# Value matmuls of attention issued one query tile later, behind the next tile's scores

## The reference

```python
x = x + mamba(_layernorm(x), ...)
x = x + _L0_ffn_ref(_layernorm(x), w_gate, w_up, w_down)   # silu(x wg) * (x wu), then wd
x = x + _L0_attn_b_ref(_layernorm(x), W)
x = x + _L0_ffn_ref(_layernorm(x), w_gate, w_up, w_down)

def _L0_attn_b_ref(x, W):          # x: (8, 2048, 1024)
    kv = x @ W.T
    K, V = (kv[..., :d], kv[..., d:])
    scores = jnp.einsum('bqd,bkd->bqk', x, K) + mask     # causal
    attn = jax.nn.softmax(scores, axis=-1)
    return x + jnp.einsum('bqk,bkd->bqd', attn, V)
```

## Time and profile before

| | |
|---|---|
| time, median of 2 runs | 3401.28 us (3397.95 to 3404.62) |
| the profiled execution | 3400.72 us |
| its span, slowest core (core 4) | 3399.1 us; cores 3373.0 to 3399.1 |
| mean granted TensorE clock, core 4 | 0.785 of 2.4 GHz |
| PE, DVE, ACT, POOL busy | 59%, 28%, 23%, 10% of the span |
| DMA | 233.31 MB, mean 69 GB/s |

### The profile page before, as it was taken

One profiled execution on the slowest core, in us unless ns is written; L12 is line 12 of the kernel. 1 busy time (PEld: TensorE's weight loads), 2 busy tenths in 40 slices (PEclk: granted clock), 3 DMA queues, 4 the chain that ended last, 5 costly groups with the idle time before them and its releaser, 6 DMA issues.

```text
span 3399.1 us, 29902 instructions; the slowest of 8 cores (3373.0 to 3399.1 us)
## 1 busy us (share of the span) xinstructions
PE 2007.9 (59%) x9275; PEld 982.9 (29%) x9432; DVE 956.2 (28%) x1617; ACT 776.6 (23%) x1196; POOL 323.4 (10%) x404
## 2 busy tenths in 40 slices
PE   0355555555555530664958678119767486859587
PEld 0233333333333210321423233114333232324232
DVE  3234444444444430011112120444322121211120
ACT  0244545445454423200101010110000110101010
POOL 0211212112121210021000000000000000000000
PEclk9576676676766755886988989559888698989889
DMA  7200000000000029334030212450211503030303
GB/s 239 78 13 25 1 25 1 25 25 1 25 1 25 22 93 287 112 113 144 8 109 8 78 47 62 156 180 2 75 62 50 182 26 99 16 108 1 112 12 96
DMA packets 69851, 233.31 MB, mean 69 GB/s; under 512 B 8450, under 2 KB 8578, under 8 KB 67652
## 3 DMA queue, kind: packets, MB, share of 16 engines
q10 hardware_dynamic: 35712, 112.21, 9.9%
q1 hardware_dynamic: 27460, 91.92, 8.8%
q0 software_dynamic: 6528, 27.27, 2.0%
HBM read 170.55 MB, written 60.82 MB: 68 GB/s over the span
## 4 chain that ended last, share of the span: by engine, by line
PE 38%; DMA 21%; DVE 13%; ACT 9%; issue 8%; DVEq 4%; POOLq 2%; POOL 2%; ACTq 2%; SPq 0%
PE ps_s L975 15%; DMA arena<-wd_c 6%; PE ps_s L941 5%; DVEq L143 4%; DMA arena<-xs 3%; PE ps_s L1045 3%; PE ps L1322 3%; PE ps L1045 3%; POOLq L143 2%; ACT L679 2%; POOL arena L560 2%; DVE arena L516 2%; PE ps L759 2%; PE ps_s L1266 2%; PE ps_s L1223 2%
## 5 line engine op out<-in xcount | busy, mean ns | idle before, releaser
L975 PE MATMUL ps_s<-arena 128*128 128x512 bf16 x2256 | 506.6, 385 | 10.8 <-DVE arena L328 8.6
L584 PE MATMUL ps_s<-arena 128*128 128x256 bf16 x1024 | 213.7, 397 | 339.1 <-ACT arena L508 336.0
L318 PE MATMUL ps<-arena 128*128 128x128 bf16 x512 | 63.5, 307 | 481.8 <-DVE arena L307 481.8
L975 PEld LDWEIGHTS ps_s<-arena 128*128 128x128 bf16 x2304 | 227.9, 99 | 288.1 <-issue 25.0
L1045 PE MATMUL ps_s<-arena 128*128 128x512 bf16 x752 | 207.9, 396 | 149.2 <-DMA arena<-wd_c 95.4
L266 ACT ACTIVATE arena<-arena 128x1024 bf16<-128x1024 f32 x64 | 67.6, 1056 | 910.8 <-DMA arena<-xs 820.9
L584 PEld LDWEIGHTS ps_s<-arena 128*128 128x128 bf16 x1024 | 137.2, 138 | 408.5 <-issue 356.1
L941 PE MATMUL ps_s<-arena 128*128 128x512 bf16 x752 | 172.3, 390 | 119.7 <-ACT arena L951 60.4
L499 PE MATMUL ps_s<-arena 128*128 128x256 bf16 x1024 | 173.7, 343 | 110.6 <-DVE arena L447 63.9
L990 DVE TENSOR_TENSOR arena<-arena,ps_s 128x512 bf16<-128x512 f32 x144 | 99.0, 688 | 422.5 <-ACT arena L984 422.5
L1045 PE MATMUL ps<-arena 128*128 128x512 bf16 x752 | 209.5, 400 | 1.0 <-issue 0.2
(11 more groups left out here) (93 smaller groups left out, 2380.4 us busy)
## 6 DMA issues: line engine op xcount, KB each, us to landing
xs<-arena ACTq DMA_DIRECT2D x48, 512.0 KB, 2.9
arena<-xs ACTq DMA_DIRECT2D x48, 512.0 KB, 4.6
arena<-wd_c SPq DMA_DIRECT2D x84, 256.0 KB, 2.6
arena<-wd_c ACTq DMA_DIRECT2D x84, 256.0 KB, 2.6
arena<-wg_t SPq DMA_DIRECT2D x16, 768.0 KB, 6.2
arena<-wu_t SPq DMA_DIRECT2D x16, 768.0 KB, 6.5
arena<-x ACTq DMA_DIRECT2D x16, 512.0 KB, 4.3
arena<-w_in ACTq DMA_DIRECT2D x8, 1024.0 KB, 10.0
```

The source lines that it names most:

```text
L318: lambda e, s=xn_bf_tile, dj=dj, pbf=pbf: e.transpose(pbf[:, dj * P:(dj + 1) * P], s[:, dj * P:(dj + 1) * P], g_ident),
L584: lambda e, dj=dj, ci=ci, bkx=bkx, half=half, par=par: e.matmul(psb[bkx][:, half * TCM:(half + 1) * TCM], win_bf[:, dj * 4096 + ci * P: dj ...
L975: lambda e, hi=hi, dj=dj, bk=bk, par=par, wsrc=wsrc: e.matmul(psb[bk], wsrc[:, dj * H + hi * P: dj * H + (hi + 1) * P], fxnt[par][:, dj * ...
```

## The change

The value matmuls, the two output operations and the store of a tile move into a function `attn_av(qj)`, and it is called one iteration later: inside iteration qi for tile qi - 1, behind the reciprocal of qi and ahead of the transposes of qi; for the last tile it is called behind the loop. What the later call needs (the marks of the copy, of the reciprocal and of the `xpn` load) is kept in `qstate`. The reciprocal of each tile now has a column of its own in `g_recip`. The single `a_probt` suffices, because the value matmuls of qi - 1 still stand ahead of the transposes of qi on TensorE.

```diff
-            mk_av_ev = None
-            mk_av67 = None
+            mk_av_ev = [None]
...
+            qstate = {}
+
+            def attn_av(qj):
+                slotj = qj % 2
+                mk_pt, mk_rcj, mk_xpnij = qstate[qj]
+                for half in range(2):
+                    bk = 6 + half
+                    for ci in range(qj + 1):
+                        em.op("tensor",
+                              lambda e, ci=ci, half=half, bk=bk, qj=qj: e.matmul(
+                                  psb[bk],
+                                  a_probt[:, ci * P:(ci + 1) * P],
+                                  a_v[:, ci * 1024 + half * 512: ci * 1024 + (half + 1) * 512],
+                                  start=(ci == 0), stop=(ci == qj)),
+                              wait=([mk_pt, mk_av_ev[0]] if (ci == 0 and half == 0) else ()),
+                              inc=([(s_pe, 1)] if (ci == qj and half == 1) else ()))
+                mk_av = s_pe.mark()
+                for half in range(2):
+                    em.op("vector",
+                          lambda e, half=half, slotj=slotj, bk=6 + half: e.scalar_tensor_tensor(
+                              a_xout[slotj][:, half * 512:(half + 1) * 512],
+                              psb[bk], g_recip[:, qj:qj + 1],
+                              a_xpni[slotj][:, half * 512:(half + 1) * 512],
+                              op0=ALU.mult, op1=ALU.add),
+                          wait=[mk_av, mk_rcj, mk_xpnij, mk_xout_free[slotj]],
+                          inc=[(s_ve, 1)], drain=(half == 0))
+                mk_av_ev[0] = s_ve.mark()
+                prev_xpni[slotj] = mk_av_ev[0]
+                mk_xout_free[slotj] = dma(
+                    "scalar", dst3[qj * P:(qj + 1) * P, :], a_xout[slotj][:],
+                    sd_st[slotj], wait=[mk_av_ev[0]])
+
             for qi in range(NT):
...
-                em.op("vector", lambda e: e.reciprocal(g_recip[:, 0:1], g_rsum[:, 0:1]),
+                em.op("vector",
+                      lambda e, qi=qi: e.reciprocal(
+                          g_recip[:, qi:qi + 1], g_rsum[:, 0:1]),
                       wait=[mk_exp], inc=[(s_ve, 1)], drain=False)
                 mk_rc = s_ve.mark()
+                if qi >= 1:
+                    attn_av(qi - 1)
                 ngr = (qi + 1 + 7) // 8
...
                 mk_probt_ev = mk_ptr_ev
-                for half in range(2):
-                    bk = 6 + half
-                    for ci in range(qi + 1):
...
-                mk_xout_free[slot] = dma(
-                    "scalar", dst3[qi * P:(qi + 1) * P, :], a_xout[slot][:],
-                    sd_st[slot], wait=[mk_av_ev])
+                qstate[qi] = (mk_probt_ev, mk_rc, mk_xpni)
+            attn_av(NT - 1)
```

## The result

The changed kernel takes 3325.32 us (median; 3319.12 us at the lowest), the kernel before, run beside it, 3405.05 us; the ratio is 0.9765, 95% interval 0.9749 to 0.9782. That is 80 us less (0.0235 x 3405), forecast were 83.5; the time lies inside the range of 3302 to 3346 us. The profiled executions are 3400.72 us before and 3319.58 us after, 81.1 apart.

What follows compares the result with a forecast made beforehand. No engine bounds the whole program; attention took 245.7 us, with TensorE pauses and low clock. Matmuls 128.5 plus 9.4, 1.9, 16.2, 1.7 and 4.5 give 162.2, 83.5 less: 3401.3 - 83.5 = 3318 us, range 3302 to 3346.

Steps and rivals of the forecast that it cites:

- Softmax wait: TensorE's wait ahead of the transposes, now covered by the previous tile's value matmuls: 56.6 us falls to 9.4 us.
- Copy wait: TensorE's wait for the copied probabilities ahead of the value matmuls, covered by the next scores: 14.9 us falls to 1.9.
- The wait that grows: Tiles 8 to 15: second transpose group waits for the first copy, queued behind output operations; 0.94 becomes 2.03 us, 16.2 in all.
- ScalarE's queue: The previous tile's store is issued behind exp: costed at nothing, up to 0.5 us in the first tiles.
- The end: Behind attention, the second feed-forward's weight and input loads move earlier as a block, neither helped nor hindered.
- Rival D: Behind attention, where all cores fetch weights and inputs together, half the gain is lost: 3360 us, chance 0.05.
- The clock: Low clock left in attention: 3.7 us in the first four tiles, 0.8 in the late ones, together 4.5 us.
- B: Late attention tiles: pauses of 2.03 us still lower the clock in all eight, 27.2 us; 3344 us, chance 0.10.
- A: The forecast itself: attention pauses mostly gone and clock held, own range 3306 to 3332 us, chance 0.80.
- C: In attention the clock is lowered because all cores are dense at once: 32 us, 3350 us, chance 0.03.
- E: The clock falls in attention's first tile and stays low for the stage: 278 us, time 3434 us, chance 0.02.

Runs made afterwards that it cites:

- experiment 2: The changed kernel with the two output operations of the tile before placed behind the copies on VectorE: 3311.34 us, attention 155.0 us.
- experiment 5: The changed kernel with one output operation, or both, done twice in tiles 8 to 15: 3330.05 us, and 3401.26 us (held up behind attention); attention 178.4 and 186.5 us.
- two-bank kernel: The changed kernel with the second group of transposes in the free bank 5: 3297.24 us, attention 143.5 us; second run 3296.37 us, ratio 0.9682.
- experiment 1: The kernel before, with unused extra matmuls filling the softmax pause of each tile: 3381.04 us, ratio 0.9886, attention 218.5 us.

## Why the prediction was right

By its own steps, for the profiled core 0:

1. Softmax wait: forecast 9.4 us, measured 8.4. The form was right (nothing from tile 9 on). Tile 1 has 1.02 instead of 1.76, since its two value matmuls ran at the low clock (1.06 us instead of 0.43) and so covered more; a fall of the clock partly pays for itself where PE covers a fixed chain.
2. Copy wait: forecast 1.9, measured 1.5.
3. The wait that grows: forecast eight times 2.03, measured eight times 1.9 to 2.0, 16.0 in all, and experiment 2 shows the cause as it was put.
4. ScalarE's queue: no pause of PE is longer than steps 1 to 3 account for; nothing, as costed.
5. The end: the loads follow the last output operation by 0.2 us as before, and the mean from there to the end is 1.3 us shorter. Rival D falls.
6. The clock: the loss was forecast at 4.5 us. 162.9 less 128.5, 8.4, 1.5, 16.0 and 1.7 leaves 6.8 us; counted in windows it is 6.1. Its two halves were both off, and in opposite ways: 3.7 us were put on the first tiles, measured 1.5, and 0.8 on the late ones, measured 4.6 (mean of the cores 5.4). That the sum came so near is in part luck. The late half failed at the step that the pauses of 2.03 us "lie below 2.35, so I expect the clock to hold from tile 4 on". In tiles 8 to 14 the clock fell behind 13 of the 56 such pauses of the eight cores, and in the last tile on all eight; on core 0 the last 32 value matmuls took 9.63 instead of 6.9 us. The trace of before held the warning, on cores that I had not read. Timeline and window of core 0, tile 2, then of core 3, tile 3:

```profile
2422.38 0.33 PE L1304 MATMUL ps<-arena 128*128 128x128 bf16 x3 [2.11 <-ACT arena L1287]
...
2423.00:2427.00 4.00, 3.58 (x9) 0.57 0.07 27
...
2421.58 0.59 PE L1304 MATMUL ps<-arena 128*128 128x128 bf16 x4 [2.35 <-ACT arena L1287]
...
2422.00:2426.00 4.00, 3.22 (x10) 0.50 0.13 49
```

Pauses of 2.11 and of the very 2.35 us lowered the clock there. One pause on one core is no threshold.

The sum was 162.2 us for a stage that took 162.9 (mean of the cores 164.0). The time fell by 80 instead of 83.5 us; 0.7 of the rest is the stage, and the 2.8 us by which attention starts later would cover what remains, which no run tells apart from scatter.

The rivals: B was half right. Pauses of 2.03 us do lower the clock, but behind 21 of 64 and not behind all, and it was priced at 27 us, a low stretch of 6.8 us for each, read off the pauses of before. Those were long pauses followed by further pauses, for transposes and for copies; between dense stretches even 3.79 us cost 1.7 us on the average (experiment 5). At that price, 13.4 us instead of 27.2, B would have given 3331 us, inside A's own range.

C, all cores dense at once, and the limit that the Trainium skill (TensorE: Matmul & The Clock Gate, Part 1) gives for dense matmuls on three or more cores of a die: in the profiles of the change and of the two-bank kernel it does not show. With two banks the 22 value matmuls of tile 10 take 4.91 us, 0.22 each, where 13/16 of the clock would give an estimated 0.27. The prediction's 0.95 on cores 5 and 7 was no sign of it either: their attention began at 2388.6 and 2389.8 us, inside that window, and up to 2388 both stand at 1.00. But the level exists on this chip. In the second execution of experiment 5, while a feed-forward matmul line (L975) runs dense on core 0 and on core 6, the windows are:

```profile
2820.00:2860.00 40.00, 39.79 (x183) 1.00 0.00 1
...
2820.00:2860.00 40.00, 39.74 (x151) 0.81 0.00 1
```

The first is core 0, the second core 6; core 7 is at 0.81 as well, and cores 4 and 5 of the same die reach 1.00 from 2830 us on. So there the trace agrees with the 13/16, though not with the whole die going down together. Levels other than 0.5 and 1.0 thus do occur, against what is said ahead of the prediction; the other eleven profiles show no stretch at 0.81. What sets it off here stays open.

E had no beginning: the clock was back at the full level by tile 2 or 3 on every core.

The assumption behind the whole sum, that 36.5 us of the old stage were low clock, holds in kind and in size: the count in windows gives 36.0 us for the same core and 38.0 for the mean, and filling the pauses gave back 28.3 us (experiment 1) with 6.7 us of loss left.

## What to carry to other kernels

In a loop where TensorE waits for a chain on other engines, count the wait twice: by itself, and by the low clock of the matmuls behind it; here the order change brought some 53 us of cover and some 30 us of clock. When work is moved so that TensorE no longer waits, look at what the move does to the order of the evacuating engine's queue and to single buffers: the one shared transpose bank cost 7.5 us before and 20.5 after, and freeing it takes two lines. Price a relapse of the clock from pauses that stand as isolated as those you will have, not from a stage that pauses three times a tile, and read it on all cores: the same pause lowers the clock on one and not on the next.

## What was not expected of the hardware

A pause of 3.13 us inside dense matmuls is in some tiles followed by full speed (32 matmuls in 6.22 us) and in others by a short low stretch (31 in 7.99 us), with the same program on the same core. A pause of 2.02 us lowered the clock in 13 of 56 cases in tiles 8 to 14, but on all eight cores in the last tile, where a pause of 1.05 us follows it. That second pause is not the whole cause: on core 0 the 8 transposes between the two already take 0.81 us instead of 0.61. Why the last tile falls each time stays open. And repeating one output operation of 0.75 us behind a drain of VectorE made the wait behind it 1.11 us longer, 0.37 us of it idle.
